# Softmax attention: the products for the maxima are issued ahead of the products for the probabilities

## What is computed

```python
mixed = x @ Wqkv.T                      # q, k, v; 16 heads of 16 channels, 4 batches of 512 tokens
attn = jnp.einsum('gqd,gkd->gqk', q, k) * norm
attn = jax.nn.softmax(attn, axis=-1)
ctx = jnp.einsum('gqk,gkd->gqd', attn, v)
```

## Time and profile before

| | |
|---|---|
| median of 3 runs | 1204.1 us (1202.74 to 1205.73) |
| profiled execution, its own time | 1201.73 us |
| its span in the trace | 1199.9 us |
| mean granted TensorE clock | 0.979 |
| PE busy | 1131.8 us (94%) |
| DVE busy | 923.5 us (77%) |
| ACT busy | 772.1 us (64%) |
| POOL busy | 634.6 us (53%) |

### The profile page before, as it was taken

The page is one execution under the profiler, slowest core; times in us unless marked ns, Lnnn a source line. Parts: engine busy times, 40 slices in busy tenths (PEclk is TensorE's granted clock), DMA queues, the critical chain, the costliest instruction groups (busy, mean ns, idle before and its releaser), DMA issues. The chain is left out here.

```text
span 1199.9 us, 22451 instructions
## 1 busy us (share of the span) xinstructions
PE 1131.8 (94%) x7558; PEld 909.3 (76%) x7558; DVE 923.5 (77%) x2124; ACT 772.1 (64%) x1533; POOL 634.6 (53%) x1078
## 2 busy tenths in 40 slices
PE   8999999888977999999999999999999999999768
PEld 7444434337646899999999999999999999999646
DVE  6888877846437788888888888888888888888452
ACT  3377767772436776777676777676777777776323
POOL 4020500001703777786777786777787687767520
PEclk9899999998989999999999999999999999999989
DMA  6434434401111012101110201111211211111020
GB/s 181 54 54 55 54 54 55 54 2 37 77 34 56 31 47 68 47 32 51 63 47 32 82 32 47 67 48 32 81 35 45 76 38 43 35 47 33 16 70 1
DMA packets 23449, 60.50 MB, mean 50 GB/s; under 512 B 3367, under 2 KB 8359, under 8 KB 22183
## 3 DMA queue, kind: packets, MB, share of 16 engines
q1 hardware_dynamic: 23335, 59.07, 18.9%
HBM read 44.67 MB, written 2.33 MB: 39 GB/s over the span
## 5 line engine op out<-in xcount | busy, mean ns | idle before, releaser
L1679 DVE SCALAR_TENSOR_TENSOR ln_xn<-l_proj_q,par,ln_xn 128x511 f32<-128x511 f32 (+2 forms) x192 | 142.6, 742 | 113.1 <-ACT ln_xn L1595 110.8
L688 DVE TENSOR_REDUCE a_neg_max<-a_scores 128x1 f32<-128x512 f32 x244 | 155.1, 683 | 38.6 <-PE a_scores L416 36.8
L607 ACT ACTIVATE a_probs<-a_scores_t 128x512 f32<-128x512 f32 x256 | 138.4, 600 | 61.0 <-PE a_scores_t L435 60.0
L1601 ACT ACTIVATE ln_xn<-ln_xn,par 128x512 f32<-128x512 f32 x128 | 92.5, 723 | 91.2 <-DVE ln_xn L1679 91.2
L1421 POOL TENSOR_TENSOR l_k_tok<-l_normed,k_norm 128x384 f32<-128x384 f32 x64 | 64.9, 1014 | 157.9 <-ACT l_normed L1612 157.9
L1679 DVE SCALAR_TENSOR_TENSOR ln_xn<-l_proj_k,par,ln_xn 128x511 f32<-128x511 f32 (+2 forms) x192 | 143.0, 745 | 4.5
L1612 ACT ACTIVATE l_normed<-l_turn_q,l_shift,l_scale 128x128 f32<-128x128 f32 x256 | 96.3, 457 | 26.1 <-POOL l_shift L1413 26.0
L1411 POOL TENSOR_TENSOR l_scale<-l_small,l_minus_half 128x8 f32<-128x8 f32 x64 | 105.0, 1641 | 5.0
L1612 ACT ACTIVATE l_normed<-l_turn_k,l_shift,l_scale 128x128 f32<-128x128 f32 x256 | 97.1, 481 | 0.0
L1555 PE MATMUL l_outp<-l_masked,l_values 128*128 128x128 f32 x512 | 88.6, 275 | 0.9 <-DVE x_tok L1707 0.9
L1654 ACT ACTIVATE l_gate<-l_proj_gv 128x512 f32<-128x512 f32 x64 | 38.2, 597 | 79.0 <-PE l_proj_gv L1477 79.0
(11 more groups left out here) (321 smaller groups left out, 3606.9 us busy)
## 6 DMA issues: line engine op xcount, KB each, us to landing
l_keep<-keep_rows SPq DMA_DIRECT2D x64, 448.0 KB, 3.6
a_stack<-a_dense SPq DMA_DIRECT2D x90, 128.0 KB, 5.1
head_raw<-w_heads SPq DMA_DIRECT2D x8, 1024.0 KB, 6.7
x_tok<-x SPq DMA_DIRECT2D x4, 512.0 KB, 8.6
wo_raw<-w_o SPq DMA_DIRECT2D x1, 2048.0 KB, 11.4
out<-x_tok SPq DMA_DIRECT2D x1, 1920.0 KB
a_stack<-a_max_rows_t SPq DMA_DIRECT2D x64, 4.0 KB
ctx_tok<-w_qkv SPq DMA_DIRECT2D x1, 768.0 KB, 7.0
```

What stands on the lines that cost most here:

```text
L607: act.activation(probs[:, n % 2, h, :], scores_t[(4 * n + h) % TURNS][:], ACT.Exp, scale=SOFT_SCALE).then_inc(probs_done, 1)
L688: dve.tensor_reduce(neg_max[:, g % 2, at:at + 1], max_bank(g, j), AX.X, ALU.max, negate=True).then_inc(max_done, 1)
L1601: act.activation(conv[:, w, m, :], conv[:, w, m, :], ACT.Silu, bias=par[:, h, 2 * TAPS + w:2 * TAPS + w + 1]).then_inc(act_sem[w], 1)
L1679: ins = dve.scalar_tensor_tensor(conv[:, w, m, s:], proj[w][:, 0:SEQ - s], par[:, h, tap:tap + 1], conv[:, w, m, s:], ALU.mult, ALU.add)
```

## The change

In each half of a slot the two calls of `max_scores` now stand before the call of `probs_chunk`. Nothing is added or removed.

```diff
@@ -549,11 +549,11 @@
             for slot in range(groups * chunks + lag):
                 s, c, n = slot // chunks, slot % chunks, slot - lag
                 for half in range(2):
-                    if n >= 0:
-                        probs_chunk(n // chunks, n % chunks, half)
                     if s < groups:
                         for e in range(2):
                             max_scores(s, c * max_per_chunk + 2 * half + e)
+                    if n >= 0:
+                        probs_chunk(n // chunks, n % chunks, half)
                     if half == 0:
                         if n >= 1:
                             context(n - 1)
```

## The result

The changed kernel takes 1209.29 us (median of 5 runs, 1208.05 to 1210.81) against 1204.1 us for the kernel before (1199.63 to 1206.34 in the five runs that were set against it): a ratio of 1.005, with a 95% interval of 1.0028 to 1.0072. It is slower by 5.2 us, 3.4 to 8.7 by the interval; the forecast was 6.7. Its profiled execution took 1208.05 us, with a span of 1206.3 us.

What follows compares the result with a forecast made beforehand. It took the softmax stage to be bound by a ring of PE and ACT, no engine full. Terms summed to +6.7 us on 1201.73, so 1208.4, or 1210.8 for a median; range +3.6 to about +12, chance 0.60.

Steps and rivals of the forecast that it cites:

- What bounds the kernel: Softmax stage: no engine full; a ring of PE and ACT, where PE work before the instruction awaiting a result is free.
- What one pair costs, 0.34 us: Each half: a pair takes 0.33 to 0.34 us of PE, so probabilities go 0.34 later and maxima 0.34 sooner.
- The bare ring, 2.01: Ten light places, mostly chunks 0 and 1: context starts 2.01 us into the half instead of 1.94; +0.7 in all.
- Chunk 2, projection gate, 6 x 0.34 = 2.0: Chunk 2 of s = 1 to 6: L372 waits through a copy behind the exponentials and pays all 0.34; +2.0 us.
- Chunks 3 to 5, 7 x 0.28 = 2.0: s = 1 to 7: behind L393 the probabilities queue behind waiting maxima, so chunk 5's context comes 0.28 later; +2.0 us.
- Context copied, 2.0: Chunk 7 of s = 0, 2, 4, 6, 7 and chunk 3 of s = 7: copy L614 delays the next context 0.34; +2.0.
- Values, 0.7: Chunk 6 of s = 1, 3, 5: L385 behind L597 moves 0.34, of which about 0.11 is slack; +0.7 us.
- A gain, -1.0: Three places in s = 6 and 7: maxima now go under the wait for the DMA of the maxima, -0.34 each; -1.0.
- The clock, 0: Softmax stage: a fall of PE's granted clock may cost up to 2.4 us, but none was put into the sum.
- Rival (a): Three group ends with the DMA wait: PE stands longer, the clock falls more; +13.9 us, 1218.0; chance 0.12.
- Rival (b): Softmax stage: later probabilities are mostly absorbed, just chunk 2's gates pay and the gains hold; +1.0 us, 1205.1; chance 0.21.
- (c): Softmax stage: DVE sets the pace, so sooner maxima make it faster; -7.0 us, 1197.1; chance 0.07.

Runs made afterwards that it cites:

- e8: Kernel before, order unchanged, but the exponential taken of 256 of the 512 queries (all in the first two chunks): 1198.36 us, ratio 0.9946.
- e9: Changed kernel, but the exponential taken of 256 of the 512 queries (all in the first two chunks): 1201.05 us, ratio 0.9968 to the kernel before.
- e5: Kernel before, order unchanged, but each maximum taken over 256 of the 512 keys: 1198.22 us, ratio 0.9937.
- e6: Changed kernel, but each maximum taken over 256 of the 512 keys: 1204.2 us, ratio 0.9988 to the kernel before.
- e3: Kernel before, with the maxima pair first only in the first half of chunk 2 of s = 1 to 6: 1202.31 us, ratio 0.9993.
- e11: Changed kernel, but the second half of chunk 4 of s = 1 to 7 keeps probabilities first: 1207.89 us, ratio 1.0055 to the kernel before.
- e4: Kernel before, with maxima first only in the first half of chunk 6 of s = 6 and chunks 2 and 6 of s = 7: 1204.28 us, ratio 1.0007.
- e7: Changed kernel, but the first half of slot 8 (s = 1, chunk 0) keeps probabilities first: 1207.36 us, ratio 1.0039 to the kernel before.
- e1: Kernel before, with the maxima pair first in the first half of each slot only: 1208.4 us, ratio 1.0037.
- e2: Kernel before, with the maxima pair first in the second half of each slot only: 1209.34 us, ratio 1.0051.
- e12: Changed kernel, but the second half of chunk 6 of s = 2 and 4 keeps probabilities first: 1207.45 us, ratio 1.0050 to the kernel before.

## Why the prediction was right, and where it was not

- **What bounds the kernel**: right as far as the order goes. Its price hangs on the exponentials; e8 and e9 show it, and e5 and e6 rule out VectorE's waits as the cause. But the stage is not a ring over ACT alone: with T first, half the reductions make it as much faster as half the exponentials.
- **What one pair costs, 0.34 us**: too large. PE starts the pairs 0.34 apart, but the exponential starts 0.23 to 0.24 later and the reduction 0.23 sooner. The start of a matmul was taken for the arrival of its result. All the terms below inherit this. The sign that DVE's idle for L416 would shrink failed too (36.8 to 37.0).
- **The bare ring, 2.01**: 1.95, so about 0.01 a place instead of 0.07; the +0.7 is at most about 0.1.
- **Chunk 2, projection gate, 6 x 0.34 = 2.0**: the mechanism is as predicted, in the changed kernel and alone in e3; the size is 0.23, +1.4.
- **Chunks 3 to 5, 7 x 0.28 = 2.0**: +0.25 in six groups and nothing in s = 7, +1.5. That L670 hardly moves was right, and the new wait behind L393 is there. But e11 shows that queueing T behind M is not the whole of it; undone, 0.07 of 0.25 comes back.
- **Context copied, 2.0**: at chunk 7 of s = 6, where the context stood behind the copy in the earlier trace rows, it is 2.44 us from the half's start against 2.21, +0.23 and not 0.34; twice the same in s = 7. At the ends of groups 2 and 4 the step "PE runs on into the wait of the first M pair for the restacking DMA, which absorbs this" failed. From L393 of chunk 4 to the next one 13.27 us became 14.48 in s = 2; less the 0.24 of the item above that is 0.97, where one 0.34 was counted, and s = 4 against e3 gives 0.95. Of it 0.80 lies at the copy, where a second M waits and holds up T: worked out for chunk 4, this was overlooked in chunk 6. The 0.95 us wait of the earlier trace rows was no cushion to count on: in s = 2 of the same trace, and in s = 4 of e3, there is none. In s = 6, where the wait for the DMA is there (0.54 before, 1.03 after), the predicted absorption holds: the 0.23 is given back before the next L393. Together about +2.4, and +0.5 in s = 0, which is in the beginning below.
- **Values, 0.7**: in the odd groups the chunk with the values is 0.20 longer from context to context (3.24 to 3.44), 3 x 0.20 = +0.6.
- **Last half, 0.3**: its context comes 1.91 after the start against 1.67, +0.24.
- **A gain, -1.0**: mostly absent. In the changed kernel chunk 2 of s = 7 is 0.31 shorter from context to context, the other two places are the same within 0.03; in e4 alone it is 0.08.
- **Not in the sum**: the beginning. L393 in chunk 0 of s = 1 came 0.98 us later than before, and still 0.58 later in e7. And in s = 1 and 3 chunks 0 to 3 pay 0.45 and not 0.23, nearly all of it in chunk 2. These are groups in which DVE also takes the statistics L77, and M pairs wait there; that this is the cause is argued, not shown.
- **The clock, 0**: right on balance by luck. The fall in s = 5 of the profile before (16.09 us from chunk 0 to 4, against about 15.1 at full clock) is gone and one in s = 1 came (17.68 against 15.73 in s = 3), +1.0 net. Rival (a) expected more falls at the ends of groups with the DMA wait; this one came behind a wait of M for VectorE. Its price of 2.4 us a fall was misread: the two stretches of the earlier trace rows are cut at different places. From L393 to L393 the groups s = 3 and s = 5 take 29.78 and 30.59. The trace of the kernel before also has falls at 33 and 272 us, which the prediction left out when it spoke of one.
- **The late DMA, not seen as such**: in s = 4 it made the kernel before 1.3 us longer than e3 at that place. The trace of the changed kernel has nothing like it, so the two traces differ by that much less than the order costs.
- **The range**: its low end, 1204.3, was named as the gates of chunk 2 alone; by the prediction's own terms these give 1204.1 + 2.0 = 1206.1, or 1205.1 with the gains. Nothing hung on it.

So the sum came close to the measured 6.7 us of the trace because its errors cancel, and that is luck. Too large were the bare ring (0.6), the gates (0.6) and chunks 3 to 5 (0.5). Too small were the copies (0.4: 1.3 at the two group ends, less 0.9 in the other places) and, by the gain that did not come, 0.7 more. The beginning (1.0) and s = 1 and 3 (0.4) were missing; the clock (+1.0) and the late DMA (-1.3) nearly cancel. Some 0.3 us of the difference is left unexplained. Rival (b), that a late T is absorbed, is refuted by the groups; (c) by e1, e2 and e6.

## What to carry to other kernels

Between producers that share an in-order engine, put first the one whose consumer is waited for next, and judge by what comes behind in the queue and not by who shows the most idle time: 43 us of waits in front of M came with a stage 6.7 us longer, and halving the work behind them left the price of the order almost as it was, while halving the exponentials took most of it away. Take the shift of a result from the starts of its consumers. Before counting on a wait as a cushion look at the same place in the other rounds of the loop and in other executions; one row may not come again. The same holds for a fall of the clock: what goes with one edit may be gone without it. No order tried here beats the kernel before.

## What the runs showed of the hardware

The kernel before varied from 1197.78 to 1209.78 us over 29 runs, and the granted clock goes with it. Its four fastest runs (1197.8 to 1200.6 us) had a mean clock of 0.981, its three slowest 0.973 to 0.975; 24 of the 29 lie below the 0.979 of the profiled execution. In e3 0.982 or 0.983 mostly means 1201.2 to 1202.3 us, 0.977 means 1206.39.

From 43 us to the end of the stage the falls to the lower level last 3.4 or 6.8 us in these traces. One of 3.4 us cost 1.0 us in the kernel before (s = 5). One of 6.8 us cost 1.9 us in the changed kernel (s = 1, against s = 3) and 2.6 in e7 behind its last L393 (18.62 us to the last context, against 15.98 in the changed kernel, which has no fall there). They were seen behind PE waits of 0.95 and 1.63 us (for a DMA) and 1.10 us (for VectorE), but not behind every wait of that length: 1.03 us at the end of s = 6 in the changed kernel, 1.08 and 1.09 us at slot 8 in e11 and e12, and 1.48 us at the end of s = 6 in e9 were followed by none.
